# Attention on one core: the output product in three rounded passes, with the updates split by ScalarE and GpSimd

## The reference, cut to what matters

```python
q, k = sigmoid(q), sigmoid(k)                      # 8 heads of 32
sink_incoming   = 1 / ((q + EPS) . (sum k + EPS) + EPS)
source_outgoing = 1 / ((k + EPS) . (sum q + EPS) + EPS)
conserved_sink   = (q + EPS) . (sum(k * source_outgoing) + EPS) + EPS
conserved_source = clip((k + EPS) . (sum(q * sink_incoming) + EPS) + EPS, -1, 1)
kv = einsum('bhnd,bhne->bhde', k, v * softmax(conserved_source) * n)
...
x_update = (q @ kv) * sink_incoming * sigmoid(conserved_sink)
t = t + x_update @ W_proj.T + b_proj
```

## Time and profile before

| what | value |
|---|---|
| time, median of 3 runs | 5421.32 us (5418.6 to 5423.04) |
| profiled execution, its own time | 5428.35 us |
| its span in the profile | 5426.6 us |
| TensorE matmul busy | 5245.8 us (97%) |
| VectorE busy | 3927.7 us (72%) |
| ScalarE busy | 2458.1 us (45%) |
| GpSimd busy | 2491.1 us (46%) |
| mean granted TensorE clock | 0.982 |

### The profile page before, as it was taken

The page is one execution under the profiler, slowest core; times in us unless marked ns, Lnnn a source line. Parts: engine busy times, 40 slices in busy tenths (PEclk is TensorE's granted clock), DMA queues, the critical chain, the costliest instruction groups (busy, mean ns, idle before and its releaser), DMA issues. The chain is left out here.

```text
span 5426.6 us, 88825 instructions
## 1 busy us (share of the span) xinstructions
PE 5245.8 (97%) x26936; PEld 3653.4 (67%) x26936; DVE 3927.7 (72%) x6063; ACT 2458.1 (45%) x4678; POOL 2491.1 (46%) x1381
## 2 busy tenths in 40 slices
PE   9999999997999999999998999999989999988999
PEld 6777655554555555555556777777667777765999
DVE  6666566666999999999995666666635666665887
ACT  4444478784344334333334555555532222211555
POOL 0000044443999999999995554555301111111332
PEclk9999999998999999999999999999999999998999
DMA  3222167775444444444446666666533333423443
GB/s 109 88 88 71 42 195 218 220 220 167 150 151 148 150 151 148 150 151 148 149 134 181 198 203 195 196 203 196 163 106 99 103 113 107 120 82 93 122 123 113
DMA packets 349116, 782.55 MB, mean 144 GB/s; under 512 B 43433, under 2 KB 147845, under 8 KB 339460
## 3 DMA queue, kind: packets, MB, share of 16 engines
q1 hardware_dynamic: 326596, 703.91, 43.9%
q10 hardware_dynamic: 22400, 77.08, 4.0%
HBM read 420.49 MB, written 360.38 MB: 144 GB/s over the span
## 5 line engine op out<-in xcount | busy, mean ns | idle before, releaser
L890 POOL TENSOR_TENSOR co_prod<-co_cross 111x512 f32<-111x512 f32 x448 | 849.8, 1897 | 0.0
L824 ACT ACTIVATE co_y_out<-co_y_ps 112x512 f32<-112x512 f32 x448 | 268.0, 598 | 927.3 <-PE co_y_ps L770 922.6
L887 POOL TENSOR_TENSOR co_prod<-co_direct 111x512 f32<-111x512 f32 x448 | 577.0, 1288 | 203.1 <-PE co_y_ps L770 115.1
L864 DVE TENSOR_TENSOR co_direct<-co_v_ps,co_spec 111x1024 f32<-111x1024 f32 x448 | 543.7, 1214 | 91.8 <-PE co_v_ps L135 87.5
L1974 POOL TENSOR_TENSOR at_t<-at_t,at_p_bias 112x1024 f32<-112x1024 f32 x56 | 137.7, 2472 | 900.1 <-DMA at_t<-t_tiles 900.1
L866 DVE TENSOR_TENSOR co_cross<-co_v_ps,co_spec 111x1024 f32<-111x1024 f32 x448 | 541.9, 1210 | 0.0
L135 PE MATMUL co_v_ps<-co_v_high,co_col_fwd_high 112*111 112x512 f32 x896 | 506.1, 565 | 1.5 <-DVE co_cross L866 1.4
L768 PE MATMUL co_y_ps<-co_prod,co_col_inv 111*112 111x512 f32 x896 | 458.2, 592 | 0.0
L770 PE MATMUL co_y_ps<-co_prod,co_col_inv 111*112 111x512 f32 x896 | 457.5, 592 | 0.1
L844 DVE TENSOR_TENSOR co_v_low<-co_v_in,co_v_high 112x1024 fp32r<-112x1024 f32 x224 | 372.5, 1663 | 0.0
L135 PE MATMUL co_v_ps<-co_v_low,co_col_fwd_high 112*111 112x512 f32 x896 | 354.3, 395 | 0.0
(11 more groups left out here) (269 smaller groups left out, 14135.3 us busy)
## 6 DMA issues: line engine op xcount, KB each, us to landing
v_rows<-pr_rows_out SPq DMA_DIRECT2D x56, 1792.0 KB, 8.2
co_v_in<-v_rows SPq DMA_DIRECT2D x448, 224.0 KB
y_rows<-co_y_out SPq DMA_DIRECT2D x448, 224.0 KB
mx_y_in<-y_rows SPq DMA_DIRECT2D x224, 448.0 KB, 5.4
kr_x_in<-x SPq DMA_DIRECT2D x56, 448.0 KB, 3.7
kern_rows<-kr_rows_out SPq DMA_DIRECT2D x28, 896.0 KB, 4.7
pr_x_in<-x SPq DMA_DIRECT2D x112, 224.0 KB
mx_x_in<-x SPq DMA_DIRECT2D x56, 448.0 KB, 5.3
```

Of the source, the lines that this page charges most:

```text
L824: nc.scalar.activation(y_out[:, b, :], y_ps[b % 2][:2 * SIDE, :], ACT.Copy).then_inc(y_ready, 1)
L864: nc.vector.tensor_tensor(direct[b % 2][:], v_ps[b % 2][:POINTS, :], spec[i][:, :2 * WIDE], ALU.mult).then_inc(real_terms, 1)
L887: nc.gpsimd.tensor_tensor(prod[b % 2][:, :WIDE], direct[b % 2][:, :WIDE], direct[b % 2][:, WIDE:], ALU.subtract).then_inc(real_ready, 1)
L890: nc.gpsimd.tensor_tensor(prod[b % 2][:, WIDE:], cross[b % 2][:, :WIDE], cross[b % 2][:, WIDE:], ALU.add).then_inc(combined, 1)
```

## The change

`kv_out` and the updates are each held as two fp32r tiles, a rounded high part and a remainder, and `output(j)` goes through `product`: high x high, high x low, low x high. ScalarE rounds each half of an update (`high_update`), GpSimd subtracts it from `upd_t` to get the remainder (`low_update`), and VectorE makes the remainder of `kv_out`. TensorE's `output(j)` waits for `upd_low`. The factors are spread two chunks ahead: update(0), unit, update(1), then for each j update(j+2), output(j), unit. GpSimd adds the bias of the first three chunks ahead of the first remainder, and that of chunk j from 3 on right behind the remainder of chunk j. SyncE's queue stays.

```diff
--- before.py
+++ after.py
@@ -1822,7 +1822,8 @@
         z_part, z_inv, z_factor = T.sb("z_part", [COMPACT, 1]), T.sb("z_inv", [128, HALVES]), T.sb("z_factor", [128, HALVES])
         gram = T.sb("gram", [128, HALVES, CH])
         kv = T.sb("kv", [128, HALVES, 128])
-        kv_out = T.sb("kv_out", [128, HALVES, CH])
+        kv_out = [T.sb(f"kv_out_{part}", [128, HALVES, CH], F32R) for part in ("high", "low")]
+        upd_parts = [[T.sb(f"upd{i}_{part}", [128, HALVES, CHUNK], F32R) for part in ("high", "low")] for i in range(2)]
         upd_t = [T.sb(f"upd_t{i}", [128, HALVES, CHUNK]) for i in range(2)]
         scratch = T.sb("scratch", [128, CHUNK])
         t1 = [T.sb(f"t1{i}", [TILE, TILES, CH]) for i in range(HELD)]
@@ -1843,6 +1844,7 @@
              "spread_mm", "sum_ready", "kept_mm", "link", "alloc_ready", "source_ready", "turn_mm", "turned", "z_mm", "key_mm",
              "key_scaled", "gram_mm", "gram_ready", "kv_mm", "kv_out_mm", "kv_out_ready", "fb_mm", "upd_ready", "proj_mm",
              "t1_biased", "t2_ready", "measured", "stats_stored"))
+        kv_out_low, upd_high, upd_low = (T.sem(n) for n in ("kv_out_low", "upd_high", "upd_low"))
         n_loaded, tok_loaded = ([T.sem(f"{n}{i}") for i in range(2)] for n in ("n_loaded", "tok_loaded"))
         t1_loaded, t2_stored = ([T.sem(f"{n}{i}") for i in range(HELD)] for n in ("t1_loaded", "t2_stored"))
         UNITS, UPDS, SUMS = CHUNKS * BLOCKS, CHUNKS * HALVES, CHUNKS * TILES // 2
@@ -1968,11 +1970,24 @@
                 nc.gpsimd.memset(sel[:], 0.0).then_inc(cleared, 1)
                 pool.wait_ge(consts_in, 16 * (len(loads) + 1))
 
+                def add_bias(im, j):
+                    pool.wait_ge(t1_loaded[j % HELD], (im.b * T1_USES[j % HELD] + j // HELD + 1) * 16)
+                    nc.gpsimd.tensor_tensor(t1[j % HELD][:], t1[j % HELD][:],
+                                            p_bias[:].unsqueeze(1).to_broadcast([TILE, TILES, CH]), ALU.add).then_inc(t1_biased, 1)
+
+                def low_update(im, j):
+                    for h in range(HALVES):
+                        pool.wait_ge(upd_high, im.b * UPDS + j * HALVES + h + 1)
+                        nc.gpsimd.tensor_tensor(upd_parts[j % 2][1][:, h, :], upd_t[j % 2][:, h, :],
+                                                upd_parts[j % 2][0][:, h, :].bitcast(F32), ALU.subtract).then_inc(upd_low, 1)
+
                 def back(im, front, beyond):
+                    for j in range(HELD):
+                        add_bias(im, j)
                     for j in range(CHUNKS):
-                        pool.wait_ge(t1_loaded[j % HELD], (im.b * T1_USES[j % HELD] + j // HELD + 1) * 16)
-                        nc.gpsimd.tensor_tensor(t1[j % HELD][:], t1[j % HELD][:],
-                                                p_bias[:].unsqueeze(1).to_broadcast([TILE, TILES, CH]), ALU.add).then_inc(t1_biased, 1)
+                        low_update(im, j)
+                        if j >= HELD:
+                            add_bias(im, j)
 
                 over_images(pool, back)
 
@@ -2045,16 +2060,16 @@
                         spread_rows(fb_ps[at:at + HALVES], j, range(HALVES)).then_inc(fb_mm, 1)
 
                     def output(j):
-                        pe.wait_ge(upd_ready, b * UPDS + HALVES * (j + 1))
+                        pe.wait_ge(upd_low, b * UPDS + HALVES * (j + 1))
                         for pair in range(TILES // 2):
                             n = j * TILES // 2 + pair
                             if n >= 2:
                                 pe.wait_ge(t2_ready, b * SUMS + n - 1)
                             for t in (2 * pair, 2 * pair + 1):
                                 for h in range(HALVES):
-                                    last = nc.tensor.matmul(proj_ps[n % 2][:TILE, (t % 2) * CH:(t % 2 + 1) * CH],
-                                                            upd_t[j % 2][:, h, t * TILE:(t + 1) * TILE], kv_out[:, h, :],
-                                                            start=h == 0, stop=h == HALVES - 1)
+                                    last = product(nc, proj_ps[n % 2][:TILE, (t % 2) * CH:(t % 2 + 1) * CH],
+                                                   [part[:, h, t * TILE:(t + 1) * TILE] for part in upd_parts[j % 2]],
+                                                   [part[:, h, :] for part in kv_out], start=h == 0, stop=h == HALVES - 1)
                             last.then_inc(proj_mm, 1)
 
                     pe.wait_ge(upd_ready, b * UPDS)
@@ -2104,13 +2119,14 @@
                     last.then_inc(kv_out_mm, 1)
                     update(0)
                     units(22)
-                    pe.wait_ge(kv_out_ready, b + 1)
-                    for j in range(1, CHUNKS):
-                        update(j)
-                        output(j - 1)
-                        if j < 6:
-                            units(22 + j)
-                    output(CHUNKS - 1)
+                    update(1)
+                    pe.wait_ge(kv_out_low, b + 1)
+                    for j in range(CHUNKS):
+                        if j + 2 < CHUNKS:
+                            update(j + 2)
+                        output(j)
+                        if j < 5:
+                            units(23 + j)
 
                 for u in range(UNITS):
                     unit(Image(0, 0), u)
@@ -2172,13 +2188,23 @@
                     sigmoids(20, 21)
                     act.wait_ge(kv_out_mm, b + 1)
                     act.wait_ge(proj_mm, b * SUMS)
-                    nc.scalar.activation(kv_out[:].rearrange("p h c -> p (h c)"), kv_out_ps[:], ACT.Copy).then_inc(kv_out_ready, 1)
-                    sigmoids(22, 23)
-                    if beyond:
-                        high_part(ahead.after(), 0)
-                    sigmoids(24, 25, 26, 27)
-                    if beyond:
-                        high_part(ahead.after(), 1)
+                    nc.scalar.activation(kv_out[0][:].rearrange("p h c -> p (h c)"), kv_out_ps[:], ACT.Copy).then_inc(kv_out_ready, 1)
+
+                    def high_update(j):
+                        if j >= 2:
+                            act.wait_ge(proj_mm, b * SUMS + (j - 1) * TILES // 2)
+                        for h in range(HALVES):
+                            act.wait_ge(upd_ready, b * UPDS + j * HALVES + h + 1)
+                            nc.scalar.activation(upd_parts[j % 2][0][:, h, :], upd_t[j % 2][:, h, :], ACT.Copy).then_inc(upd_high, 1)
+
+                    high_update(0)
+                    sigmoids(22)
+                    high_update(1)
+                    for j in range(CHUNKS - 2):
+                        high_update(j + 2)
+                        sigmoids(23 + j)
+                        if beyond and j in (0, 4):
+                            high_part(ahead.after(), j // 4)
 
                 first = Image(0, 0)
                 high_part(first, 0)
@@ -2319,7 +2345,7 @@
                         dve.wait_ge(fb_mm, b * CHUNKS + j + 1)
                         for h in range(HALVES):
                             if j >= 2:
-                                dve.wait_ge(proj_mm, b * SUMS + (j - 1) * TILES // 2)
+                                dve.wait_ge(upd_low, b * UPDS + (j - 2) * HALVES + h + 1)
                             nc.vector.tensor_tensor(upd_t[j % 2][:, h, :], fb_ps[j % 2 * HALVES + h][:, :CHUNK],
                                                     qk[:, h, j * CHUNK:(j + 1) * CHUNK], ALU.mult).then_inc(upd_ready, 1)
 
@@ -2340,19 +2366,22 @@
                                                     proj_ps[n % 2][:TILE, :].rearrange("p (t c) -> p t c", t=2),
                                                     t1[j % HELD][:, 2 * pair:2 * pair + 2, :], ALU.add).then_inc(t2_ready, 1)
 
+                    take_update(0)
+                    dve.wait_ge(kv_out_ready, b + 1)
+                    nc.vector.tensor_tensor(kv_out[1][:].rearrange("p h c -> p (h c)"), kv_out_ps[:],
+                                            kv_out[0][:].rearrange("p h c -> p (h c)").bitcast(F32), ALU.subtract).then_inc(kv_out_low, 1)
+                    take_update(1)
                     for j in range(CHUNKS):
-                        take_update(j)
-                        if beyond and j == 4:
+                        if j + 2 < CHUNKS:
+                            take_update(j + 2)
+                        if beyond and j == 2:
                             low_part(ahead.after(), 0)
-                        if j:
-                            add_residual(j - 1)
-                            if front and j == CHUNKS - 1:
-                                sum_tokens(ahead)
-                            measure(j - 1)
-                    add_residual(CHUNKS - 1)
-                    if beyond:
-                        low_part(ahead.after(), 1)
-                    measure(CHUNKS - 1)
+                        add_residual(j)
+                        if front and j == CHUNKS - 2:
```

(4 more changed lines are left out.)

## The result

12 runs of each kernel: 5428.64 us after (5422.52 to 5435.6), 5419.58 before (5410.96 to 5423.04). The ratio is **1.0019, 95% interval 1.0012 to 1.0027**: slower by some 9 us where 5 us less was forecast. The two profiled executions would say the opposite, 5423.87 after and 5428.35 before. The first is the third fastest of its 12, the second is slower than all 12 runs of before: it was 3.1 us behind the other before the attention phase's first head sums (3987.04 against 3983.97), in code that is the same in both. A change of this size can't be read off one pair of executions; what they are good for is where the time lies.

The account below looks back on a forecast made before the run. TensorE, busy for 97% of the span, was taken as the bound. Seven images at -0.8 us plus 0.8 in the last gave -4.8, from the median 5421.3 to 5416.5 us; 8-in-10 range 5402 to 5437.

Parts of the forecast that it names:

- the stretch's own sum: Update stretch of an image: next image starts 36.2 us after update(0)'s first matmul, against 37.0 before, 0.8 us gained.
- The saving per output: Output product of a chunk: 24 rounded passes of 0.118 us save 0.53 us, step from 5.46 to 4.93 us.
- the start at U+4.3: Start of output(0), waiting for chunk 0's remainders: forecast 4.4 us behind U, the first matmul of update(0).
- the subtraction of 1.146 us: GpSimd's subtraction making half a chunk's remainder, 448 columns: forecast 1.15 us.
- the stand of 1.74 us at output(6): TensorE idle ahead of output(6), its remainders queued on GpSimd behind chunk 5's load-bound bias: forecast 1.8 us.
- the covered "sel": End of stretch: "sel" ready 12.3 us behind R(3), ahead of output(6)'s end at 13.8, so TensorE does not wait.
- R(3): Start of chunk 3's second residual add, right behind output(3)'s end; forecast 22.4 us behind update(0)'s first matmul, 0.35 ahead.
- Rival 1: End of stretch: the GpSimd chain holds nothing, "sel" decides; 2.4 us an image, 17 in all, 5404 us; chance 0.22.
- Rival 2: Update stretch: GpSimd's subtraction runs slower, 1.6 us for 448 columns; next image 2.8 us later, 5446 us; chance 0.10.
- everything behind it follows TensorE: After the stretch: whatever follows the next image's first matmuls moves with their start, 0.8 us earlier an image.
- Rival 3: Update stretch: stands lower TensorE's clock for one output an image, 20 us over seven images, 5437 us; chance 0.10.
- the last image: Last image, without units, going by load and bias: GpSimd's new load and the later start cost 0.8 us in all.

Follow-up runs that it names:

- Experiments 3 and 4: The changed kernel with a fourth residual tile: 5402.52 us, 0.9975; the changed kernel with one unit moved ahead of output(0): 5426.57 us, 1.0019.
- experiment 5: GpSimd's first biases held behind VectorE's split of the next image's chunk 3: changed kernel 5408.42 us, 0.9982; kernel before 5405.73 us, 0.9982.
- experiment 7: The kernel before, with GpSimd's first biases timed so that they always overlap VectorE's split of chunk 3: 5426.84 us, 1.0018.
- experiment 6: The changed kernel with first biases held, again, as base: 5409.02 us; the same with unused matmuls ahead of output(0) and output(6): 5408.71 us; both 0.9987.

## Why the prediction was wrong

**Right: the stretch's own sum.** The saving per output (0.118 us a pass, step 4.84 for 4.93), the start at U+4.3, the subtraction of 1.146 us, the stand of 1.74 us at output(6) behind a bias that waited for its load, the covered "sel". The 0.8 us of an image were 1.4: 0.4 us less up to R(3), as each chunk was 0.1 us quicker than its sum, and 0.2 less from there on, as the load was 0.1 sooner. Experiments 3 and 4 show the mechanism: with the load taken away the stand goes, with only the other stand filled nothing moves. Rival 1 is out for this reason, Rival 2 by the 1.146 us.

**Wrong: "everything behind it follows TensorE".** This is the step that failed. The prediction asked what comes next only as far as the head sums. The next front is not a rigid piece that moves with them. Its tile loads hang on VectorE's last measuring, its multiplications on TensorE. The stand at output(6) moves one against the other by 0.4 to 1.6 us, and the biases behind those loads then run into a VectorE instruction with two SBUF inputs. Measured: 18 to 20 us in the changed kernel and 12 in before (experiment 5), and +9 in before when the overlap alone is forced (experiment 7). The rule was even at hand: the prediction quoted the shared interface and asked which VectorE work of the **stretch** it would hit, not what the GpSimd instructions that change place meet elsewhere. So was the case itself: the 1.83 us of idle time that Rival 3 took from image 2 of before were TensorE's wait behind such a held split, and the prediction did not ask where they came from.

**Half right: Rival 3, at 0.10.** The clock does fall behind stands under 2 us. But it was priced at a whole output at the lower level in every image, 20 us; it comes in one to three of seven and costs 1.6 us each time. The sum should have carried 2 to 5 us of it. That 5428.6 lies inside the wide range of 5402 to 5437 is therefore luck: its upper end was held open for 20 us of clock in the stretches, not for what happened. As a cause of the loss it counts mostly in the fronts, where a held-up split brings it.

**Mis-sized: the last image.** 0.8 us forecast, 2.4 measured from U to the statistics in the two first traces (37.9 before; 40.4 and 40.5 after), and with biases held before takes 36.2, the changed kernel 40.5 in experiment 5 and 38.4 in the base of experiment 6: 4.4 and 2.2 more. The row of before that stood for it was itself lengthened by a fall at its start, and the changed kernel has one more fall in its middle, 22.8 us behind U, in three of its four traces; the 38.4 is the trace without it. There GpSimd's queue runs without a gap from the bias of chunk 3 to the remainder of chunk 6, and TensorE waits for it ahead of output(0) (0.68 us), output(4) (2.79), output(5) (1.46) and output(6) (1.51).

Together: 9 to 11 us were lost, of which 6 to 8 go with the overlap and 2.7 stay when it is gone in both. These two parts add up by the way they were measured, and are no check on each other. In the traces with the overlap gone the stretches give -7.0 and -5.3 where the sum had -5.6, and the last image +4.4 and +2.2 where it had +0.8. So why the medians are at +2.7 there and not at -4.8 is shown in part only: 1.4 to 3.6 us of it are the last image, and the rest was not traced to a place that both pairs share.

**Open.** The first tile's bias began 6.6 us behind the issue of its load in the image of before above and 6.9 in that of the changed kernel, and over images 1 to 6 of the three traces it is 6.1 to 7.9; where such half microseconds come from was not tried, and they decide which images are hit. Nor is it shown why the clock falls behind a split of 1.7 us in three images and not in a fourth, or behind the same stand of 1.87 us in four of six. Nor did I vary the length of a stand to find from where the clock falls.

## What to carry to other kernels

When a change puts a wait into one engine's queue, list what starts the next part on each of the other engines, and see which of them now starts earlier against the one that waits; an overlap that was missed by half a microsecond is as much a part of the schedule as a wait. A two-input GpSimd instruction of 2.4 us beside two-input VectorE work can hold that work up for nearly its own length (2.2 us here): give it a place by a semaphore instead of leaving it to a load. And fill a stand only after you have looked whether it is the one that ends last.

## What the hardware showed that I had not expected

The granted clock fell to its lower level behind single waits of 1.1 us in one image and not in the next, with the same code; stands of 1.1 us at output(0) did so in none to five of seven images per execution. A fall made a stretch 1.5 to 1.7 us longer, and the stretch of image 0 with two of them 3.2. And VectorE's four-element L2226 of the kernel before, 2.10 us in its median, takes 0.66 in the changed kernel (0.76 above, where it ends at 4351.84 and a GpSimd instruction at 4351.81). In all seven images of before and in all seven of the changed kernel it ends 0.02 to 0.03 us behind the GpSimd instruction that is under way. So it waits that one out, as the split does, and shorter GpSimd instructions made it faster although there are more of them.
